# Fused AdaLN-style block: three PSUM banks for the second attention's scores, and the loop turn moved

## What is computed

```python
x = x + attn(conv(x, cond))          # depthwise causal conv, 8 taps, taps from cond
x = x + ffn(cond2(x, mask=cond))     # second attention over 512 positions, then a gated FFN

# attn: 16 heads of 32, 256 positions, ALiBi and causal, fp32
scores = einsum('bqhd,bkhd->bhqk', q, k) * scale;  scores = where(causal, scores + bias, -1e9)
out = (softmax(scores) @ v) @ out_w.T + out_b
# cond2: x is read as (C=256, T=512); 16 heads of 16, 512 positions
att = einsum('bhqd,bhkd->bhqk', Q, K) / 4 + b;  att = att * m + (1 - m) * -1e30;  y = softmax(att) @ V
# ffn: gate, up, down weights are cubic splines of few control points
inter = silu(h @ gate_w.T) * (h @ up_w.T);  out = inter @ down_w.T
```

## Time and profile before

| | |
|---|---|
| median of 3 runs | 1441.94 us (1441.18 to 1443.64) |
| the profiled execution, its own time | 1434.63 us |
| its span, first to last instruction | 1432.8 us |
| mean granted TensorE clock | 0.943 of full speed |
| TensorE matmul busy | 1244.2 us, 87% |
| VectorE / ScalarE / GpSimd busy | 755.2 / 521.8 / 359.6 us |
| chain that ended last | PE 66%, DVE 12%, issue 5%, POOL 5%, SPq 5% |

### The profile page before, as it was taken

The page is one execution under the profiler, slowest core; times in us unless marked ns, Lnnn a source line. Parts: engine busy times, 40 slices in busy tenths (PEclk is TensorE's granted clock), DMA queues, the critical chain, the costliest instruction groups (busy, mean ns, idle before and its releaser), DMA issues.

```text
span 1432.8 us, 23277 instructions
## 1 busy us (share of the span) xinstructions
PE 1244.2 (87%) x8680; PEld 725.6 (51%) x8680; DVE 755.2 (53%) x1173; ACT 521.8 (36%) x698; POOL 359.6 (25%) x203
## 2 busy tenths in 40 slices
PE   4485379899889999899999999899998998999988
PEld 3152135555455555556455555555455564656445
DVE  5354463547534673457724575346733577346732
ACT  1221145323532245223542245223552235423562
POOL 3079810055000830038000650009200380000000
PEclk9697579999989999999998999799998999999999
DMA  9857722366043731256042650337222560437124
GB/s 330 236 197 204 220 83 59 98 159 185 6 105 120 175 106 46 61 164 215 22 104 82 145 173 15 91 124 193 84 54 53 165 214 22 104 124 189 62 104 162
DMA packets 80495, 181.12 MB, mean 126 GB/s; under 512 B 14404, under 2 KB 54292, under 8 KB 70708
## 3 DMA queue, kind: packets, MB, share of 16 engines
q1 hardware_dynamic: 78352, 175.21, 41.9%
q0 software_dynamic: 1280, 4.20, 1.1%
q10 hardware_dynamic: 768, 0.26, 0.1%
HBM read 106.41 MB, written 21.14 MB: 89 GB/s over the span
## 4 chain that ended last, share of the span: by engine, by line
PE 66%; DVE 12%; issue 5%; POOL 5%; SPq 5%; DMA 4%; ACT 2%; DVEq 0%; ACTq 0%; POOLq 0%
PE psum L1054 8%; PE psum L848 8%; PE psum L1004 7%; PE psum L890 6%; DVE max L760 5%; PE psum L891 4%; PE psum L892 4%; PE psum L854 4%; SPq L374 3%; PE psum L879 3%; PE psum L868 3%; PE psum L916 3%; PE psum L1040 3%; PE psum L973 2%; PE psum L938 2%
## 5 line engine op out<-in xcount | busy, mean ns | idle before, releaser
L760 DVE TENSOR_REDUCE max<-psum 128x1 f32<-128x512 f32 x512 | 329.0, 685 | 113.0 <-PE psum L1004 110.9
L619 ACT ACTIVATE probs<-psum 128x1024 f32<-128x1024 f32 x256 | 248.8, 1022 | 119.0 <-PE psum L1040 118.3
L1004 PE MATMUL psum<-k,q 52*128 52x512 f32 x512 | 169.9, 514 | 75.4 <-DVE max L760 49.8
L505 POOL TENSOR_TENSOR h<-h_in,tap 128x1024 f32<-128x1024 f32 x7 | 13.3, 1900 | 701.3 <-DVE low L674 701.3
L1004 PEld LDWEIGHTS psum<-k,q 52*128 52x128 f32 x512 | 65.2, 191 | 197.8 <-DVE max L760 136.3
L580 ACT ACTIVATE probs<-psum 128x1024 f32<-128x1024 f32 x64 | 62.1, 1022 | 211.8 <-PE psum L959 211.8
L1054 PE MATMUL psum<-probs,v 128*32 128x256 f32 x2048 | 138.7, 389 | 0.4 <-ACT probs L619 0.3
L848 PE MATMUL psum<-h,qkv_w 128*128 128x256 f32 x512 | 119.8, 389 | 18.0 <-DVE h L653 18.0
L515 POOL TENSOR_TENSOR h<-h,products 128x1024 f32<-128x1024 f32 x49 | 128.0, 2611 | 3.8
L848 PEld LDWEIGHTS psum<-h,qkv_w 128*128 128x128 f32 x512 | 96.4, 193 | 39.1 <-issue 26.6
L890 PE MATMUL psum<-stack 128*128 128x512 f32 x256 | 113.7, 444 | 1.3 <-DVE stack L693 1.2
(11 more groups left out here) (106 smaller groups left out, 1722.9 us busy)
## 6 DMA issues: line engine op xcount, KB each, us to landing
stack<-wd_sorted SPq DMA_DIRECT2D x64, 1024.0 KB, 5.8
stack<-high SPq DMA_DIRECT2D x128, 128.0 KB, 2.4
stack<-low SPq DMA_DIRECT2D x64, 128.0 KB, 2.4
q<-high SPq DMA_DIRECT2D x128, 64.0 KB, 3.4
k<-high SPq DMA_DIRECT2D x128, 64.0 KB, 2.3
wd_sorted<-stack SPq DMA_DIRECT2D x8, 1024.0 KB, 4.5
h_in<-in_x_lanes SPq DMA_DIRECT2D x9, 512.0 KB, 4.7
x<-in_x_rows SPq DMA_DIRECT2D x8, 512.0 KB, 5.8
```

The source lines that it names most:

```text
L619: nc.scalar.activation(probs[:, u // 2 % 2, u % 2 * 2:u % 2 * 2 + 2, :], psum[:, 2 + u % 2 * 2:4 + u % 2 * 2, :], ACT.Exp)\
L760: nc.vector.reduce_max(max2[:, g, e, i, t:t + 1], psum[:, s % 2, :], AX_X).then_inc(S["s2_max"], 1)
L1004: nc.tensor.matmul(psum[:, e, :], r(q2[rows, g, i, t * P:(t + 1) * P]), r(k2[rows, g, i, :]), start=True, stop=True).then_inc(S["s2_ready" ...
```

## The change

- Scores of the output pass use banks 0, 1 and 7 in turn (`SCORE_BANKS`; bank 7 not in round 5), three before the values and one behind. A score waits for the last maximum in its own bank; the first in bank 7 waits for `max2_low` 2, those from round 5 on for `y_out` 1. `turn(g)` stands before the round's scores on TensorE and VectorE.
- `values2` covers 512 columns in one matmul instead of two of 256.
- The first attention's scores, their transpose and `values(1)` form `scores1(b)`, called at the end of the batch before, so ahead of the loop's branch. `S1_BANKS` are (3, 0), and `v1_out` is waited for at the third head. One mask matmul over two diagonal blocks replaces two, since no maximum reads the block between.
- In batch 0 the sort uses four slots; all eight gathers are issued before the convolution; each store stands before a stack's copies on SP; VectorE sorts four tiles first and one after each of the next four window steps.

```diff
+SCORE_BANKS = [s % 2 for s in range(WINDOW_SCORES)]
+for _k in range(1, 1 + (NS - WINDOW_SCORES) // 4):
+    for _s in range(4):
+        _free = (0, 1) if _k in TURN_AT and _k in OUT_AT else (0, 1, 7)
+        SCORE_BANKS.append(min(_free, key=lambda x: len(SCORE_BANKS) - 1 - SCORE_BANKS[::-1].index(x)
+                               if x in SCORE_BANKS else -1))
+LAST_IN_BANK = [max((r for r in range(s) if SCORE_BANKS[r] == SCORE_BANKS[s]), default=None) for s in range(NS)]
-S1_BANKS = (0, 3)
+S1_BANKS = (3, 0)
-def round_pair(k, i):
-    first = WINDOW_SCORES + 4 * (k - 1) + 2 * i
-    return range(first, min(first + 2, NS))
+def round_scores(k, i):
+    first = WINDOW_SCORES + 4 * (k - 1)
+    return range(first + 3 * i, min(first + 3 + i, NS))
...
+                def store_sorted(n):
+                    sp.wait_ge(down_low, n + 1)
+                    sp.dma_start(wd_dram[n], stack1[:, n % SORT]).then_inc(sorted_stored[n % SORT], 16)
                 def stacks2(g):
                     for off, stack, blocks in ((0, q2, QUERY_BLOCKS), (1024, k2, KEY_BLOCKS)):
+                        if first:
+                            store_sorted(2 * g + off // 1024)
...
-                    for n in range(RING):
+                    for n in range(NT):
                         gather(n)
...
-                    if first and k > TAPS - 1 - (NT - RING):
-                        gather(k)
...
+                for n in range(SORT if first else 0):
+                    sort(n)
                 for n in range(NT + 1):
...
+                    if first and 0 < n <= NT - SORT:
+                        sort(SORT - 1 + n)
...
-                    if n == 0:
+                    if n == 2:
                         wait("v1_out", 1)
...
-                    nc.tensor.matmul(bank[:, 0:L], ident_b[:], mask_q[:], start=False, stop=False,
-                                     skip_group_check=True)
-                    last = nc.tensor.matmul(bank[:, L + P:2 * L], ident_b[:], mask_q[:, 0:P], start=False, stop=True,
+                    last = nc.tensor.matmul(bank.rearrange("p (a n) -> p a n", n=P)[:, 0:LT * LT:3, :], ident_b[:],
+                                            mask_q[:, None, :].broadcast_to([P, 2, P]), start=False, stop=True,
                                             skip_group_check=True)
...
                     if s < 2:
                         wait("v2_out", CT)
+                    elif LAST_IN_BANK[s] is None:
+                        wait("max2_low", 2)
                     else:
-                        wait("s2_max", s - 1)
+                        wait("s2_max", LAST_IN_BANK[s] + 1)
+                    if SCORE_BANKS[s] == 7 and s >= WINDOW_SCORES + 4 * (OUT_AT[0] - 1):
+                        wait("y_out", 1)
...
-                        last = nc.tensor.matmul(psum[e * BLK:(e + 1) * BLK, 6, queries], v2[:, kt, head, :],
-                                                probs[:, kt % 2, e, queries], start=kt + half == 0, stop=kt == CT - 1,
+                        last = nc.tensor.matmul(psum[e * BLK:(e + 1) * BLK, 6, :], v2[:, t, head, :],
+                                                probs[:, t % 2, e, :], start=t == 0, stop=t == CT - 1,
                                                 skip_group_check=True)
...
-                    for s in round_pair(k, 0):
-                        scores(s)
                     if k in TURN_AT:
                         turn(TURN_AT.index(k) + 1)
-                    for j in range(2):
-                        values2(2 * (k - 1) + j)
+                    for s in round_scores(k, 0):
+                        scores(s)
+                    values2(k - 1)
                     if k in OUT_AT:
                         turn_outputs(OUT_AT.index(k))
-                    for s in round_pair(k, 1):
+                    for s in round_scores(k, 1):
                         scores(s)
...
                 turn_outputs(NG - 1)
+                if not last_batch:
+                    scores1(b + 1)
```

## The result

The changed kernel takes **1385.3 us** (median of 4 runs, 1382.3 to 1393.4) against 1441.6 (1436.2 to 1443.6) for the kernel before in the same comparison: a ratio of 0.962, interval 0.958 to 0.966, 56 us less. Predicted were 1369 (range 1352 to 1394) and 73.5 us less. The time also lies 3 us outside the forecast's own range of 1356 to 1382, in the band that the prediction had let in for rivals B and C.

A forecast was written before the change was run, and what follows sets the result against it. TensorE, busy 87% of the span, was taken to bound the kernel by its work plus the holes between instructions. 37 + 17 + 3.5 + 16 = 73.5 off 1434.6, plus 7.3, gave 1368.4, stated as 1369; range 1352 to 1394.

The forecast's parts named there:

- B: Rival, output pass: stalls in rounds 1 and 5 eat the shorter rounds, three banks give nothing; 1386 us, chance 0.13.
- C: Rival, first batch: the sort of the down weights stays as slow; 1385 us, chance 0.12.
- Loop turn: Between batches: the branch's fetch hides beside values(1), removing TensorE's hole and lower clock; 37 us, low end 33.
- rival A: Loop turn: the hole moves behind values(1) and the clock falls again over t1; 1402 us, chance 0.12.
- Three banks: Output pass, rounds 1 to 8: fewer waits for VectorE's maxima; 2.1 us a batch, 17 in 8.
- the walk: Output pass, rounds 1 to 9 stepped through with trace constants: values 2.47 to 4.32 us apart, 27.74 against 29.85.
- rival D: Output pass: waits of 0.9 to 1.3 us in rounds 1 and 5 lower the clock; slower, 1539 us, chance 0.03.
- Mask matmul: scores1: one mask matmul less shortens the loop of TensorE and VectorE; 0.45 us a batch, 3.5 in 8.
- Halves: Output pass: values as four matmuls of 512 columns instead of eight of 256; 0, at most 0.1 us a round.
- First batch: Batch 0's sort: earlier gathers and stores bring the first shifted matmul to 173, 16 us earlier, range 6 to 22.
- dips in the output pass: Sign against the forecast: the clock row showing dips in the output pass would mean the prediction was wrong.
- Near 15.5 in all seven: Sign for the loop turn: stretch from last output transposes to first t1 matmul near 15.5 us in all seven.

The follow-up runs named there:

- undo_banks: The changed kernel with banks 0 and 1, two scores on either side of the values and turn(g) behind the round's first scores again: 1420.5 us (0.987).
- turn_only: The kernel before with scores1 called at the end of the batch ahead, new S1_BANKS order and v1_out wait, both mask matmuls kept: 1410.2 us (0.978).
- undo_turn: The changed kernel with scores1 called at the head of its own batch again: 1403.6 us (0.975).
- undo_gather: The changed kernel with batch 0's sort as before (three slots, gathers 3 to 7 between the taps): 1392.5 us (0.969).
- aug_after: The changed kernel with VectorE making the bias rows behind its work on the first attention's maxima: 1373.5 us (0.955).
- before_aug: The kernel before with SyncE's bias-row copies ahead of the first block's output wait and VectorE's bias-row steps behind its maxima work: 1431.0 us (0.997).

## Why the prediction was right, and where it was short

- **Loop turn, 37 (low end 33).** The mechanism is right: the fetch runs beside `values(1)`, no hole of 3 us, and rival A is out for this kernel. Its two assumptions were read rightly from the earlier trace rows (start 0.15 after L940, cost about 0.1). The size was off: added to the old kernel alone it gave 27 to 31, taken from the new one 18. The step that failed is that nothing became late in its place, which the sum put at nothing. VectorE's bias rows had lain in the turn's hole; uncovered they are a hole of 1.6 to 1.8 us in scores1, with a fall of the clock behind three of seven. I had written that VectorE "is at the aug rows until later", and took it as a reason to expect nothing of two banks, not as a wait.
- **Rival A** was given 0.12. Its mechanism is real one step on: the fetch of the next block. Where the body stands in TensorE's program decides it, and the diff does not show that. The changed kernel had it favourable, undo_banks did not, for 12 to 13 of its 18.7 us.
- **Three banks, 17 (0 to 5.7 a batch).** At full clock 2.0 a batch, so the mechanism and the walk are right: its distances are right to 0.1 or so each, the late first values cost 1.5 instead of 1.23. The 16.5 by the medians agrees with the 17 in part by luck, since in the traces of before and after the term is 7.2. The walk stood at full clock, though, and the change's own stall in round 5 brought the clock down in five of seven passes, 0.9 to 2.2 us each. That is rival D's mechanism at a tenth of its price or less: the clock came back after 3.4 or 6.8 us. D had 21 us a batch.
- **Mask matmul, 3.5.** The price of its loop is right: 3.7 in scores1. That this reaches the end is not: 3.3 of it is given back between t1 and the first values, a wait that I put at nothing. **Halves, 0.** Measured 0.02 a batch in the pass.
- **First batch, 16 (6 to 22).** Measured 7 by the medians, 9 to 11 in the trace. The first scores came at 142.4 (141 predicted), the end of the stacks at 173.4 instead of 165. The failed term is the price of SyncE's copies: I took 2.50 for four high copies, the one such row; in before the eight sets took 2.5 to 4.9, 3.0 in the mean. In after they took 3.2 to 4.8, 3.8 in the mean, 10 us in all. The line was named rightly.
- **What I did not cost at all**: the first window score, +4.4, with falls of the clock behind it, +6.4. That hole stood in the trace of before at 0.64 to 1.82 us. I read only the holes that the diff closes, not those that it leaves.
- Of the signs I named, "dips in the output pass" came true and the rest of the forecast with it: dips and gain are no contradiction. "Near 15.5 in all seven" held in four (15.5 to 15.8); one took 16.4 and two 17.5 and 17.6.

Added up, the single measurements give turn 31, banks 16.5, mask 3.7 and sort 7, together 58 for 56 measured. This agreement is no proof: the turn is 18 beside the new kernel, the mask's 3.7 is from one stretch, and the terms act on each other through the clock. The measured time lies in the range only because the range had been widened for rivals B and C, which did not happen. The mechanisms of the four terms were right; what is missing went to waits and falls of the clock that the sum put at nothing, and to SyncE's copies.

## What to carry to other kernels

When a long hole goes, list what other engines did inside it: each of those is now a wait of its own, and here one of 1.4 us gave back 6 us of the turn's 37 by the medians and 14.7 in the traces. Cost every short hole that stays on a busy TensorE twice, once for its length and once for the clock behind it, and look at the clock of the stretch after it; closing or shortening three holes of 0.95 to 2.4 us a batch brought 41 us by the medians (some 6 of it in batch 0, for another reason), where the whole change had brought 56. A hole's length alone did not tell whether the clock would fall, so count how often it fell in several traces. And before a variant with a hardware loop is judged, look for an "issue" hole just behind the branch: where the body stood in the program cost 12 to 13 us here, nearly as much as the edit under test.

## What the hardware showed that I had not expected

- A taken branch on TensorE brings two fetches of 16 KB, one 0.9 to 2.6 us after it begins, one 0.7 to 1.9 us after it ends. The first is hidden by matmuls already issued (0.1 us of cost in after, against 3.7 us of branch). In undo_banks the hole before t1, with the second one in it, was 2.0 to 2.8 us longer in three turns of five, and moving the body by 20 instructions removed that.
- The granted clock fell to its lower level behind holes of 0.85 and 0.95 (output pass), 1.41 (turn_only), 1.58 and 1.76 (scores1) and 2.0 to 2.4 us (window), but not behind every such hole: in after 0.95 in two passes of seven and 1.6 to 1.8 in four of seven stretches of scores1 had none, and in four other traces (undo_turn, undo_banks, undo_gather, aug_after) a fall stood behind only 5 of 12 window holes of 2.0 us or more. In before it once fell in a pass with no hole over 0.5 us in the 8 us ahead of it (at 701.7). What besides the hole decides is open. So is how long the clock stays down once it has fallen: a turn cost 4.4 to 9.1 us in before, 4.9 to 10.9 in before_aug and 4.9 to 5.5 in undo_turn, hole and clock together.
- Where nothing was queued, the same branch left a hole of 3.5 to 4.0 us in before and 4.4 to 4.7 in undo_turn.
